# Expert down product with its operands exchanged, the gate on token rows, and attention values 65 columns wide

## Chip, cores, metric

One Trainium2 chip, one of its cores. The metric is the device time of one execution in microseconds (us), the median of the runs.

## The reference, cut to what matters

The program is two transformer layers on `x` of 32 samples × 256 tokens × 128 features, float32. The change is in the first one.

```python
# first attention: 16 query heads, 8 key/value heads of 64
out = jnp.einsum('bhgij,bhjd->bhid', attn, v)      # attn is a causal softmax
# first feed-forward: 16 experts of 64, top 4, and a shared expert of 256
def body(acc, inp):
    wu, wd, cw = inp
    y = relu2(x2 @ wu.T) @ wd.T
    return (acc + cw[:, None] * y, None)
routed, _ = jax.lax.scan(body, jnp.zeros_like(x2), (up_w, down_w, combine.T))
shared = relu2(x2 @ shared_up.T) @ shared_down.T
# and around it, gb being one value per sample and feature
x = x + gb * (routed + shared)
```

`relu2` is the square of relu, `combine` holds a token's weights for its four experts and zero for the others.

## The kernel before

`x` stays in SBUF for the whole program, token rows on the 128 partitions, 64 tiles of 128 tokens. Five stages follow one another, each a block in which every engine runs its own hand-written instruction list; between two blocks all engines meet. The stages are a setup, the first attention, the experts (`moe`), the second attention and an MLP. Semaphores order the engines inside a block.

**Experts.** The loop goes over 16 runs of two samples, 512 tokens. The 1024 hidden features of the 16 experts and the 256 of the shared expert are ten blocks of 128 (`RT` = 8 routed, `ST` = 2 shared), called units u = 0 to 9, the shared ones first. For each unit PE makes the up product into `pU` (512 token columns, `pe_up`, L1093), ACT takes relu into `r` (L1312) and squares it into `a` for a shared unit or `q` for a routed one (L1325). DVE multiplies `q` with the tokens' routing weights `cwB` into `a` (`dve_weigh`, L1238). PE then adds the down product of `a` into `pD` over all ten units (`pe_down`, L1103): the turned-down weights `dT` are loaded, `a` passes with its 512 columns, and `pD` holds features on partitions, tokens in columns. ACT scales `pD` with the gate, a value per feature and sample (`act_gate`, L1332), into `og`; PE turns `og` back to token rows in four transposes into `pB` (`pe_back`, L1110); DVE adds `pB` to `x` (`dve_add`, which calls `add_to_x`, L122) and measures mean and variance for the next layer.

The order of the work is written out by hand in the block of each engine, three runs interleaved: PE does up and down products of run n alternately (down follows up by three units), the last three down products of run n − 1 between the first three up products of run n, then the transposes of run n + 2 (`pe_front`, L1076), the router's product of run n + 2 (`pe_route`, L1084, eight passes) and `pe_back` of n − 1. `pe_down` of unit 0 waits for the gate of the run before, which frees `pD`.

**Routing weights.** DVE computes the weights of run n + 1 (`dve_scores` to `dve_weights`) and turns them into `cwT`. SP stores `cwT` to DRAM (`by_expert`, four stores, L1058), waits for them, and loads them back in four transfers of 512 KB that repeat every expert's row over 64 partitions (`cwB`, L1065). A run's store waits until the load of the run before has landed. SP issues every transfer of this stage; at its start it first calls `ahead`, which issues the ten loads of the later MLP's weights (`mlp_load`, L1813 to L1817).

**First attention.** For each sample, group of four heads and query tile, PE multiplies the softmax numerators `pr` (loaded, 128×128) with the values `va` (passing), whose columns are 64 values, then ones that give the row sum: `VW` = 66 columns, of which the last is a second one that nobody reads (`pe_weighted_values`, L450 and L451). DVE divides by the sum (`dve_outputs`).

A float32 matmul of the program is two matmul instructions in the trace, each with a weight load.

Of the kernel before, what the change touches and what calls it, by code (L numbers as in the profile page):

```python
# [14 lines left out]
P = 128  # L15
# [252 lines left out]
def attention0(nc, c, weights, later, following):  # L268
# [3 lines left out]
    with ExitStack() as ctx:  # L272
# [8 lines left out]
        VW = DH + 2  # L281
# [718 lines left out]
def moe(nc, c, weights, ahead, halve, following, products):  # L1000
# [3 lines left out]
    with ExitStack() as ctx:  # L1004
# [32 lines left out]
        og = sb('og', [D, W])  # L1037
# [8 lines left out]
        s_pz, s_pk, s_pT, s_pd, s_pm = (sem(x) for x in ('pz', 'pk', 'pT', 'pd', 'pm'))  # L1046
        block = ctx.enter_context(nc.Block())

        @block.sync
        def _(sp):  # L1050
            ahead(sp)
            for n in range(RUNS):
                sp.wait_ge(s_cT, n + 1)
                if n >= 1:
                    for part in s_cw:
                        sp.wait_ge(part, 2 * 16 * n)
                for j in range(P // SQ):
                    sp.dma_start(by_expert[:, :, j, :], cwT[SQ * j:SQ * j + E, :, :]).then_inc(s_cd, 16)  # L1058
                sp.wait_ge(s_cd, 16 * P // SQ * (n + 1))
                if n >= 2:  # L1060
                    sp.wait_ge(s_a, RT * (n - 1))
                rows = by_expert.rearrange('(k j y) t g r -> k y j (t g r)', k=2, y=2)
                for k in range(2):
                    for y in range(2):
                        sp.dma_start(cwB[n % 2][EI * y:EI * (y + 1), RT // 2 * k:RT // 2 * (k + 1), :],  # L1065
                                     rows[k, y].unsqueeze(0).broadcast_to((EI, RT // 2, W))).then_inc(s_cw[k], 16)

        def weights_of(u):
            return RT + u if u < ST else u - ST
# [25 lines left out]
        def pe_down(pe, n, u):  # L1095
            if u < ST:
                pe.wait_ge(s_sq, IT * n + u + 1)
            else:
                pe.wait_ge(s_a, RT * n + u - ST + 1)
            if u == 0 and n >= 1:  # L1100
                pe.wait_ge(s_og, n)
            t = weights_of(u)
            pe.matmul(pD[:, :], dT[:, t * D:(t + 1) * D], a[(IT * n + u) % 4][:, :], start=u == 0, stop=u == IT - 1).then_inc(s_dn, 1)  # L1103

        def pe_back(pe, n):
            pe.wait_ge(s_og, n + 1)
            if n >= 1:
                pe.wait_ge(s_st, ADD_STEPS * (n - 1) + 1)
            for t in range(T4):
                last = pe.transpose(pB[:, t * P:(t + 1) * P], og[:, t * P:(t + 1) * P], c.id32[:, :])  # L1110
            last.then_inc(s_oT, 1)

        @block.tensor
        def _(pe):
            for n in range(-2, RUNS + 1):
# [27 lines left out]
                if 0 <= n - 1 < RUNS:  # L1143
                    pe_back(pe, n - 1)
# [94 lines left out]

        def dve_add(dve, n):  # L1240
            dve.wait_ge(s_oT, n + 1)
            add_to_x(dve, c, s_st, n, T4, pB[:, :])
# [5 lines left out]
        def _(dve):  # L1248
            dve.wait_ge(weights.s_loaded, 16 * MOE_LOADS)
            dve.wait_ge(s_km, 4)  # L1250
            for n in range(-2, RUNS + 1):
# [10 lines left out]
                elif n == -1:  # L1262
                    dve_normalise(dve, 2)
                elif 1 <= n < RUNS - 2:
                    dve_normalise(dve, n + 2)
                if 0 <= n < RUNS:
# [60 lines left out]
        def act_gate(act, n):  # L1327
            if n >= 1:
                act.wait_ge(s_oT, n)
            act.wait_ge(s_dn, IT * (n + 1))  # L1330
            for m in range(S2):
                last = act.activation(og[:, m * N:(m + 1) * N], pD[:, m * N:(m + 1) * N], ACT.Copy, scale=c.mod[:, 0, 5, n * S2 + m:n * S2 + m + 1])  # L1332
            last.then_inc(s_og, 1)

        @block.scalar
        def _(act):
            for n in range(-2, RUNS + 1):
# [6 lines left out]
                if 0 <= n - 1 < RUNS:  # L1344
                    act_gate(act, n - 1)
# [862 lines left out]
```

## Time and profile before

| | us |
|---|---|
| median of 3 runs | 2060.88 (2057.25 to 2062.87) |
| profiled execution, its own time | 2060.06 |
| its span in the profile | 2058.3 |
| PE busy | 1982.2 |
| DVE busy | 1661.7 |
| ACT busy | 1432.7 |
| POOL busy | 634.5 |
| mean granted TensorE clock | 0.982 of full |

Busy times are of the profiled execution and its span; the time of an execution is what the device took for it, 1.8 us more than the span here. PE is the matmul engine (PEld its weight loads), DVE the vector engine, ACT the activation engine, POOL the general one, SP the one that issues transfers. Busy time of matmuls is modelled, as they overlap each other; what a matmul costs is read from start to start. In a timeline a row is a group of like instructions: start, length until the last has ended, engine, line, operation, output <- inputs, shapes, count, and in brackets how long the engine was idle before and what ended that.

### The profile page before, as it was taken

The page shows a single profiled execution, that of the slowest core. Times are in us where ns is not written, and L with a number is a line of the kernel's source. Part 1 is how long each engine was busy: PE and PEld are TensorE (multiplying, and loading weights), DVE is VectorE, ACT ScalarE, POOL GpSimd, SP SyncE. Part 2 cuts the span into 40 slices and gives each one's busy share as a digit, 9 for nine tenths or more (in the row PEclk, how much of TensorE's full clock was granted, in tenths as well). Part 3 has the DMA queues.
Part 4 walks back from the last instruction along what each step waited for, and adds up shares of the span by engine and source line. Part 5 has one row for each costly group of instructions (what it writes and reads, how often), then busy time and mean ns, then how long its engine had stood idle before and what let it go on. Part 6 is the DMA issues. An engine that isn't in the chain of part 4 may idle for free. (4 is left out here: it accounts for less than half of the span.)

```text
span 2058.3 us, 39519 instructions
## 1 busy us (share of the span) xinstructions
PE 1982.2 (96%) x14373; PEld 1323.9 (64%) x14373; DVE 1661.7 (81%) x3939; ACT 1432.7 (70%) x1922; POOL 634.5 (31%) x865
## 2 busy tenths in 40 slices
PE   5999999999999999999799999899999997999998
PEld 3777777777777777777444444577777773444443
DVE  5898889888888889874576676588888887999997
ACT  3877878788877888776477777567767764555554
POOL 2444554455444554453000000144444440000000
PEclk9999999999999999999799999999999997999999
DMA  2400000000000000000665455000000000000000
GB/s 88 108 20 21 22 22 11 22 22 22 12 21 22 22 21 12 22 21 11 140 125 123 103 109 124 1 2 2 2 2 2 2 2 1 16 11 17 11 17 16
DMA packets 55360, 69.33 MB, mean 34 GB/s; under 512 B 13009, under 2 KB 32641, under 8 KB 55169
## 3 DMA queue, kind: packets, MB, share of 16 engines
q1 hardware_dynamic: 55168, 66.82, 14.1%
q8 instruction: 116, 1.90, 0.4%
q14 instruction: 76, 0.61, 0.1%
HBM read 45.30 MB, written 4.72 MB: 24 GB/s over the span
## 5 line engine op out<-in xcount | busy, mean ns | idle before, releaser
L904 POOL TENSOR_SCALAR_AFFINE_SELECT pr<-pr 128x512 f32<-128x512 f32 x256 | 201.8, 812 | 371.5 <-ACT pr L827 371.5
L450 PE MATMUL a_pO<-va,pr 128*128 128x66 f32 x2048 | 303.2, 271 | 1.9 <-POOL pr L904 1.5
L450 PEld LDWEIGHTS a_pO<-va,pr 128*128 128x128 f32 x2048 | 272.3, 192 | 18.9 <-issue 15.4
L1736 ACT ACTIVATE c_pr<-c_pS 128x1536 f32<-128x1536 f32 x128 | 185.9, 1453 | 93.8 <-PE c_pS L1543 93.8
L1783 POOL TENSOR_SCALAR_AFFINE_SELECT c_pr<-c_pr 128x512 f32<-128x512 f32 x256 | 176.3, 718 | 212.2 <-DVE c_pr L1635 212.2
L793 ACT ACTIVATE sq<-a_pW 128x512 f32<-128x512 f32 x192 | 114.4, 597 | 148.5 <-PE a_pW L391 145.9
L821 ACT ACTIVATE th<-a_pS 128x1536 f32<-128x1536 f32 x128 | 186.0, 1453 | 30.1 <-PE a_pS L435 29.6
L451 PE MATMUL a_pO<-va,pr 128*128 128x66 f32 x1024 | 198.2, 275 | 0.0
L827 ACT ACTIVATE pr<-th 128x1536 f32<-128x1536 f32 x128 | 190.7, 1490 | 3.0
L435 PE MATMUL a_pS<-qs,k 128*128 128x512 f16 (+1 forms) x1024 | 187.3, 326 | 1.0 <-issue 1.0
L1103 PE MATMUL b_pD<-b_a,b_dn 128*128 128x512 f32 x320 | 165.3, 600 | 5.2 <-DVE b_a L1238 4.8
L1635 DVE TENSOR_SCALAR c_pr<-c_pr 128x1536 f32<-128x1536 f32 x128 | 130.2, 1017 | 47.6 <-ACT c_pr L1736 45.2
L1093 PE MATMUL b_pU<-b_hT,b_un 128*128 128x512 f32 x320 | 167.6, 607 | 0.0
L435 PEld LDWEIGHTS a_pS<-qs,k 128*128 128x128 f16 x1024 | 98.6, 98 | 99.9 <-issue 36.0
L1238 DVE TENSOR_TENSOR b_a<-b_q,b_cwB 128x512 f32<-128x512 f32 x128 | 87.9, 688 | 84.2 <-ACT b_q L1325 79.1
L451 PEld LDWEIGHTS a_pO<-va,pr 128*128 128x128 f32 x1024 | 155.7, 192 | 0.0
L1312 ACT ACTIVATE b_r<-b_pU 128x512 f32<-128x512 f32 x160 | 95.7, 598 | 80.1 <-PE b_pU L1093 80.1
L912 POOL TENSOR_TENSOR as<-on 128x128 f32<-128x128 f32 x256 | 116.9, 467 | 109.9 <-PE a_pW L472 95.5
L687 POOL TENSOR_TENSOR qp<-qg,qp 128x1024 f16<-128x1024 f32 x64 | 137.0, 2142 | 20.1 <-ACT qp L803 20.1
L678 DVE RECIPROCAL rl<-a_pO 128x4 f32<-128x4 f32 x256 | 44.9, 175 | 121.5 <-PE a_pO L451 121.5
L626 DVE TENSOR_TENSOR qg<-a_pW,a_gam 128x512 f32<-128x512 f32 x192 | 131.5, 686 | 10.5 <-ACT sq L793 7.8
L391 PE MATMUL a_pW<-a_wq,hT 128*128 128x512 f32 x256 | 126.8, 619 | 0.7 <-DVE qs L695 0.7
(242 smaller groups left out, 4354.1 us busy)
## 6 DMA issues: line engine op xcount, KB each, us to landing
b_cwB<-b_by_expert SPq DMA_DIRECT2D x64, 512.0 KB, 8.5
k<-k SPq DMA_DIRECT2D x64, 256.0 KB, 3.7
x<-in_L_attn_tokens_dram SPq DMA_DIRECT2D x8, 512.0 KB, 7.3
out_dram<-x SPq DMA_DIRECT2D x16, 256.0 KB, 2.3
d_h<-in_L_ffn_h_w_dram SPq DMA_DIRECT2D x2, 1024.0 KB, 7.3
b_by_expert<-b_cwT SPq DMA_DIRECT2D x64, 8.0 KB, 1.8
wmod<-in_L_wmod_dram SPq DMA_DIRECT2D x2, 384.0 KB, 3.8
d_w<-in_L_ffn_w_w_dram SPq DMA_DIRECT2D x3, 256.0 KB, 3.0
```

The costliest lines, as they stand in the source:

```text
L435: last = pe.matmul(out, kk[:, h // G2, keys * P:(keys + 1) * P], qs[k][:, h:h + G2, keys * P:N], start=first, stop=not first)
L450: pe.matmul(out, w[:, hh * N + t * P:hh * N + (t + 1) * P], v[:, 0, p, :], start=True, stop=t == 0)
L451: last = pe.matmul(out, w[:, HPG * N + hh * P:HPG * N + (hh + 1) * P], v[:, 1, p, :], start=False, stop=True)
L626: dve.tensor_tensor(qg[n % 2][:, t, cols], pW[BANK_OF[m]][:, :], gam[:, cols], ALU.mult).then_inc(s_qg, 1)
L687: eng.tensor_tensor(to[:, t, :, DH:2 * DH], x.rearrange('p (h d) -> p h d', d=DH), to[:, t, :, 0:DH], ALU.subtract).then_inc(done, 1)
L821: act.activation(th[:, :], pS[:, :], ACT.Tanh, scale=1.0 / SOFTCLAMP).then_inc(s_th, 1)
L827: act.activation(pr[g % 2][:, :], th[:, :], ACT.Exp, scale=SOFTCLAMP * DH ** (-0.5)).then_inc(s_pr, 1)
L904: last = gp.affine_select(out=part, in_=part, compare_op=ALU.is_ge, fill=0.0, base=0, pattern=[[0, HPG], [1, P]], channel_multiplier=-1)
L1093: pe.matmul(pU[(IT * n + u) % 4][:, :], uT[:, t, :], hT[n % 3][:, :], start=True, stop=True).then_inc(s_up, 1)
L1103: pe.matmul(pD[:, :], dT[:, t * D:(t + 1) * D], a[(IT * n + u) % 4][:, :], start=u == 0, stop=u == IT - 1).then_inc(s_dn, 1)
L1736: act.activation(pr[g][:, :, :], pS[:, :, 0:N + P], ACT.Exp, scale=float(1.0 / np.sqrt(np.float32(DQ)))).then_inc(s_ex, 1)
L1783: last = gp.affine_select(out=part, in_=part, compare_op=ALU.is_ge, fill=0.0, base=0, pattern=[[0, HPG], [1, P]], channel_multiplier=-1)
```

## The change

- `VW` is 65: the values have one column of ones.
- `pe_down` now loads a block of `a` (128 hidden features × 128 tokens) and passes the 128 columns of `dT`, four times per unit, one for each tile of 128 tokens. `pD` thus holds token rows on partitions, as `x` does. `pe_back` and its transposes are gone.
- The gate is then different in every column and the same on all partitions of a sample. `dve_gate` multiplies `pD` with `gb`, the gates of all 32 samples repeated on every partition (16 KB each), into `og`; `act_gate` is gone, and `dve_add` reads `og`.
- `gb` is made at the start of the stage: PE turns the gates (`pe_turn_gates`), ACT copies them (`act_take_gates`), SP stores them to DRAM (`by_sample`, 16 KB) and loads them back repeated over 128 partitions (2 MB). That load and the MLP's ten loads (`ahead`) are issued in run 0 behind the load of its routing weights.

```diff
-        VW = DH + 2
+        VW = DH + 1
...
-        og = sb('og', [D, W])
+        og = sb('og', [P, T4, D])
+        gs_, gb = sb('gates', [B, D]), sb('gb', [P, B, D])
+        by_sample = nc.dram_tensor('b_by_sample', (B, D), F32, kind='Internal').ap()
...
         @block.sync
         def _(sp):
-            ahead(sp)
+            sp.wait_ge(s_gs, 1)
+            sp.dma_start(by_sample, gs_[:, :]).then_inc(s_gd, 16)
             for n in range(RUNS):
...
+                if n == 0:
+                    sp.wait_ge(s_gd, 16)
+                    sp.dma_start(gb[:, :, :].rearrange('p b d -> p (b d)'),
+                                 by_sample.rearrange('b d -> (b d)').partition_broadcast(P)).then_inc(s_gb, 16)
+                    ahead(sp)
...
-            t = weights_of(u)
-            pe.matmul(pD[:, :], dT[:, t * D:(t + 1) * D], a[(IT * n + u) % 4][:, :], start=u == 0, stop=u == IT - 1).then_inc(s_dn, 1)
-
-        def pe_back(pe, n):
-            pe.wait_ge(s_og, n + 1)
-            if n >= 1:
-                pe.wait_ge(s_st, ADD_STEPS * (n - 1) + 1)
+            rows = weights_of(u)
             for t in range(T4):
-                last = pe.transpose(pB[:, t * P:(t + 1) * P], og[:, t * P:(t + 1) * P], c.id32[:, :])
-            last.then_inc(s_oT, 1)
+                last = pe.matmul(pD[:, t * P:(t + 1) * P], a[(IT * n + u) % 4][:, t * P:(t + 1) * P], dT[:, rows * D:(rows + 1) * D],
+                                 start=u == t == 0, stop=u == IT - 1, skip_group_check=True)
+            last.then_inc(s_dn, 1)
+
+        def pe_turn_gates(pe):
+            pe.transpose(pB[0:B, 0:D], c.mod[:, 0, 5, :], c.id32[:, :]).then_inc(s_gT, 1)
...
+        def dve_gate(dve, n):
+            dve.wait_ge(s_dn, IT * (n + 1))
+            if n == 0:
+                dve.wait_ge(s_gb, 16)
+            else:
+                dve.wait_ge(s_st, ADD_STEPS * (n - 1) + 1)
+            by = gb[:, n * S2:(n + 1) * S2, :].unsqueeze(2).broadcast_to((P, S2, TT, D))
+            dve.tensor_tensor(og[:, :, :].rearrange('p (s t) d -> p s t d', s=S2),
+                              pD[:, :].rearrange('p (s t d) -> p s t d', s=S2, t=TT), by, ALU.mult).then_inc(s_og, 1)
+
         def dve_add(dve, n):
-            dve.wait_ge(s_oT, n + 1)
-            add_to_x(dve, c, s_st, n, T4, pB[:, :])
+            dve.wait_ge(s_og, n + 1)
+            add_to_x(dve, c, s_st, n, T4, og[:, :, :].rearrange('p t d -> p (t d)'))
...
+                if 0 <= n - 1 < RUNS:
+                    dve_gate(dve, n - 1)
                 if 0 <= n < RUNS:
                     dve_weigh(dve, n, 2)
...
-        def act_gate(act, n):
-            if n >= 1:
-                act.wait_ge(s_oT, n)
-            act.wait_ge(s_dn, IT * (n + 1))
-            for m in range(S2):
-                last = act.activation(og[:, m * N:(m + 1) * N], pD[:, m * N:(m + 1) * N], ACT.Copy, scale=c.mod[:, 0, 5, n * S2 + m:n * S2 + m + 1])
-            last.then_inc(s_og, 1)
+        def act_take_gates(act):
+            act.wait_ge(s_gT, 1)
+            act.activation(gs_[:, :], pB[0:B, 0:D], ACT.Copy).then_inc(s_gs, 1)
```

The instruction lists at three places. Line numbers above 1034 are 3 to 17 higher after the change.

SP at the start of the expert stage, before: the ten MLP loads (`d_w`, `d_h` and their scales; six of them left out), then run 0's stores and loads of routing weights and run 1's stores.

```order
L1813 DMA d_w<-in_L_ffn_w_w_dram 128x4x128
L1814 DMA d_w1s<-in_L_ffn_w_s_dram 128x4x1
...
L1816 DMA d_w<-in_L_ffn_w_w_dram 128x512
L1817 DMA d_w3s<-in_L_ffn_w_s_dram 128x1
L1058 DMA b_by_expert<-b_cwT 64x1x32 [waits b_cT]
L1058 DMA b_by_expert<-b_cwT 64x1x32 x3
L1065 DMA b_cwB<-b_by_expert 64x4x512 [waits b_cd]
L1065 DMA b_cwB<-b_by_expert 64x4x512 x3
L1058 DMA b_by_expert<-b_cwT 64x1x32 [waits b_cw1,b_cw0,b_cT]
```

After:

```order
L1054 DMA b_by_sample<-b_gates 32x128 [waits b_gs]
L1061 DMA b_by_expert<-b_cwT 64x1x32 [waits b_cT]
L1061 DMA b_by_expert<-b_cwT 64x1x32 x3
L1068 DMA b_cwB<-b_by_expert 64x4x512 [waits b_cd]
L1068 DMA b_cwB<-b_by_expert 64x4x512 x3
L1072 DMA b_gb<-b_by_sample 128x4096 [waits b_gd]
L1825 DMA d_w<-in_L_ffn_w_w_dram 128x4x128
...
L1829 DMA d_w3s<-in_L_ffn_w_s_dram 128x1
L1061 DMA b_by_expert<-b_cwT 64x1x32 [waits b_cw1,b_cw0,b_cT]
```

The MLP's loads moved from ahead of run 0's routing weights to between those of run 0 and of run 1, with the gates' load in front of them.

PE at the turn from one run to the next, before: from the last down product of a run to the third of the next.

```order
L1103 MATMUL b_pD<-b_a,b_dn 128x512 [waits b_a]
L1076 MATMUL b_pX<-id,b_xn 128x128 [waits b_hT,b_xn]
L1076 MATMUL b_pX<-id,b_xn 128x128 x3
L1093 MATMUL b_pU<-b_hT,b_un 128x512 [waits b_r]
L1103 MATMUL b_pD<-b_a,b_dn 128x512 [waits b_og,b_sq]
...
L1084 MATMUL b_pR<-b_gT,b_hT 128x16 [waits b_ex,b_hT]
L1084 MATMUL b_pR<-b_gT,b_hT 128x16 x3
L1093 MATMUL b_pU<-b_hT,b_un 128x512 [waits b_r]
L1110 MATMUL b_pB<-id,b_og 128x128 [waits b_st,b_og]
L1110 MATMUL b_pB<-id,b_og 128x128 x3
L1103 MATMUL b_pD<-b_a,b_dn 128x512 [waits b_a]
```

After:

```order
L1112 MATMUL b_pD<-b_dn,b_a 128x128 [waits b_a]
L1112 MATMUL b_pD<-b_dn,b_a 128x128 x3
L1084 MATMUL b_pX<-id,b_xn 128x128 [waits b_hT,b_xn]
L1084 MATMUL b_pX<-id,b_xn 128x128 x3
L1101 MATMUL b_pU<-b_hT,b_un 128x512 [waits b_r]
L1112 MATMUL b_pD<-b_dn,b_a 128x128 [waits b_og,b_sq]
L1112 MATMUL b_pD<-b_dn,b_a 128x128 x3
...
L1092 MATMUL b_pR<-b_gT,b_hT 128x16 [waits b_ex,b_hT]
L1092 MATMUL b_pR<-b_gT,b_hT 128x16 x3
L1101 MATMUL b_pU<-b_hT,b_un 128x512 [waits b_r]
L1112 MATMUL b_pD<-b_dn,b_a 128x128 [waits b_a]
```

Each down product is four narrow ones, with the wait ahead of the first; the four transposes into `pB` are gone; the wait for `og` stays at the first down product of a run.

DVE at the same turn, before: the end of the routing weights, the normalised tokens `xn`, the weighing of u = 2 to 4 and the residual add.

```order
L1230 STREAM_TRANSPOSE b_cwT<-b_cwp 128x128 [waits b_cd,b_rt]
L112 TENSOR_SCALAR b_xn<-x,mv,rs 128x128 [waits b_xT]
L112 TENSOR_SCALAR b_xn<-x,mv,rs 128x128 x3
L1238 TENSOR_TENSOR b_a<-b_q,b_cwB 128x512 [waits b_dn,b_cw0,b_sq] x3
L122 TENSOR_TENSOR x<-x,b_pB 128x512 [waits b_oT]
```

After:

```order
L1235 STREAM_TRANSPOSE b_cwT<-b_cwp 128x128 [waits b_cd,b_rt]
L112 TENSOR_SCALAR b_xn<-x,mv,rs 128x128 [waits b_xT]
L112 TENSOR_SCALAR b_xn<-x,mv,rs 128x128 x3
L1252 TENSOR_TENSOR b_og<-b_pD,b_gb 128x512 [waits b_st,b_dn]
L1243 TENSOR_TENSOR b_a<-b_q,b_cwB 128x512 [waits b_dn,b_cw0,b_sq] x3
L122 TENSOR_TENSOR x<-x,b_og 128x512 [waits b_og]
```

The gate stands between `xn` and the weighing, and waits for the last down product.

## Rows read from the trace of the kernel before

**Rows 1.** The page, busy time of each engine with its share of the span
```profile
PE 1982.2 (96%) x14373; PEld 1323.9 (64%) x14373; DVE 1661.7 (81%) x3939; ACT 1432.7 (70%) x1922; POOL 634.5 (31%) x865
```

**Rows 2.** Windows, a steady run: length, busy, clock, DMA share, GB/s
```profile
1096.73:1115.69 18.96, 18.96 (x57) 9.19 (x56) 13.19 (x57) 14.10 (x27) 0.00 (x0) 1.00 0.53 114
```

**Rows 3.** Timeline of PE, run 0: start, length, instruction, count, idle before
```profile
1007.58 2.07 PE L1103 MATMUL b_pD<-b_a,b_dn 128*128 128x512 f32 x2 [4.79 <-DVE b_a L1238]
```

**Rows 4.** Timeline of DVE, run 0 of the experts
```profile
1006.84 2.50 DVE L1238 TENSOR_TENSOR b_a<-b_q,b_cwB 128x512 f32<-128x512 f32 x4 [4.41 <-DMA b_cwB<-b_by_expert]
```

**Rows 5.** Timeline of SP's DMA issues, start of the expert stage
```profile
981.62 0.39 SPq L1813 DMA_DIRECT2D d_w<-in_L_ffn_w_w_dram  x1
...
995.21 2.57 SPq L1058 DMA_DIRECT2D b_by_expert<-b_cwT  x4
999.02 2.61 SPq L1065 DMA_DIRECT2D b_cwB<-b_by_expert  x4
1011.71 2.49 SPq L1058 DMA_DIRECT2D b_by_expert<-b_cwT  x4
1015.45 2.58 SPq L1065 DMA_DIRECT2D b_cwB<-b_by_expert  x4
```

**Rows 6.** Timeline of PE within a steady run
```profile
1103.29 1.02 PE L1103 MATMUL b_pD<-b_a,b_dn 128*128 128x512 f32 x2
1104.15 0.96 PE L1084 MATMUL b_pR<-b_gT,b_hT 128*128 128x16 f32 x8
1104.96 1.10 PE L1093 MATMUL b_pU<-b_hT,b_un 128*128 128x512 f32 x2
1105.90 0.60 PE L1110 MATMUL b_pB<-id,b_og 128*128 128x128 f32 x4
1106.34 0.59 PE L1103 MATMUL b_pD<-b_a,b_dn 128*128 128x512 f32 x1
```

**Rows 7.** Timeline of PE in the first attention, weighted values
```profile
602.38 0.61 PE L450 MATMUL a_pO<-va,pr 128*128 128x66 f32 x4
602.83 0.39 PE L451 MATMUL a_pO<-va,pr 128*128 128x66 f32 x2
```

**Rows 8.** Timeline of PE in the second attention, value product
```profile
1314.42 0.61 PE L1530 MATMUL c_pB<-c_wv,c_hT 128*128 128x128 f32 x4
1314.86 0.55 PE L1844 MATMUL c_pS<-id,d_w 128*128 128x128 f16 x7
```

**Rows 9.** Timeline of DVE at the turn of a steady run
```profile
1101.90 0.69 DVE L1238 TENSOR_TENSOR b_a<-b_q,b_cwB 128x512 f32<-128x512 f32 x1 [2.08 <-ACT b_q L1325]
```

**Rows 10.** Timeline of ACT at the same place
```profile
1100.51 0.84 ACT L1332 ACTIVATE b_og<-b_pD,mod 128x256 f32<-128x256 f32 x2 [0.32 <-PE b_pD L1103]
```

**Rows 11.** Timeline of PE, end of the expert stage
```profile
1304.56 0.27 PE L1432 MATMUL b_pU<-id,c_dkv 128*32 128x128 f32 x1
```

**Rows 12.** Timeline of ACT, end of the expert stage
```profile
1305.44 0.36 ACT L1437 ACTIVATE c_dT<-b_pU 32x256 f32<-32x256 f32 x1
```

**Rows 13.** Timeline of DVE, run 1 of the experts
```profile
1025.07 0.69 DVE L1238 TENSOR_TENSOR b_a<-b_q,b_cwB 128x512 f32<-128x512 f32 x1 [2.76 <-ACT b_q L1325]
```

**Rows 14.** Timeline of PE, run 1 of the experts
```profile
1029.54 1.02 PE L1103 MATMUL b_pD<-b_a,b_dn 128*128 128x512 f32 x2
```

**Rows 15.** Windows of the start, the MLP load, routing load, wait's end
```profile
8.00:10.00 2.00, 1.06 (x6) 0.95 (x6) 0.95 (x5) 0.00 (x0) 0.00 (x0) 1.00 0.95 368
...
980.00:996.00 16.00, 9.36 (x29) 6.50 (x30) 9.84 (x52) 3.94 (x10) 2.25 (x11) 0.59 0.64 182
999.00:1010.00 11.00, 6.21 (x18) 3.02 (x17) 6.21 (x28) 3.91 (x9) 0.00 (x0) 0.85 0.90 185
...
1007.60:1013.40 5.80, 5.80 (x7) 2.50 (x8) 3.33 (x8) 1.23 (x2) 0.00 (x0) 0.50 0.51 99
```

**Rows 16.** DMA in 982 to 996: 40 slices' busy tenths; a load's landing
```profile
DMA  0057997999768999999667999999999864210000
...
d_w3s<-in_L_ffn_w_s_dram SPq DMA_DIRECT2D x1, 0.5 KB, 6.6
```

More of the change, by code:

```diff
@@ L1045, in moe @@
         s_og, s_oT, s_st = (sem(x) for x in ('og', 'oT', 'st'))
-        s_pz, s_pk, s_pT, s_pd, s_pm = (sem(x) for x in ('pz', 'pk', 'pT', 'pd', 'pm'))
+        s_gT, s_gs, s_gd, s_gb, s_pz, s_pk, s_pT, s_pd, s_pm = (sem(x) for x in ('gT', 'gs', 'gd', 'gb', 'pz', 'pk', 'pT', 'pd', 'pm'))
         block = ctx.enter_context(nc.Block())
@@ L1101, in pe_down @@
                 pe.wait_ge(s_og, n)
-            t = weights_of(u)
-            pe.matmul(pD[:, :], dT[:, t * D:(t + 1) * D], a[(IT * n + u) % 4][:, :], start=u == 0, stop=u == IT - 1).then_inc(s_dn, 1)
-        def pe_back(pe, n):
-            pe.wait_ge(s_og, n + 1)
-            if n >= 1:
-                pe.wait_ge(s_st, ADD_STEPS * (n - 1) + 1)
-            for t in range(T4):
-                last = pe.transpose(pB[:, t * P:(t + 1) * P], og[:, t * P:(t + 1) * P], c.id32[:, :])
-            last.then_inc(s_oT, 1)
+            rows = weights_of(u)
+            for t in range(T4):
+                last = pe.matmul(pD[:, t * P:(t + 1) * P], a[(IT * n + u) % 4][:, t * P:(t + 1) * P], dT[:, rows * D:(rows + 1) * D],
[3 more added lines that the diff above has]
+            pe.transpose(pB[0:B, 0:D], c.mod[:, 0, 5, :], c.id32[:, :]).then_inc(s_gT, 1)
         @block.tensor
         def _(pe):
+            pe_turn_gates(pe)
             for n in range(-2, RUNS + 1):
@@ L1142, in _ @@
                     pe_up(pe, n, 5)
-                if 0 <= n - 1 < RUNS:
-                    pe_back(pe, n - 1)
                 if n == RUNS:
@@ L1325, in act_square @@
             act.activation(to[:, :], r[(IT * n + u) % 4][:, :], ACT.Square).then_inc(s_sq, 1)
-        def act_gate(act, n):
-            if n >= 1:
-                act.wait_ge(s_oT, n)
-            act.wait_ge(s_dn, IT * (n + 1))
-            for m in range(S2):
-                last = act.activation(og[:, m * N:(m + 1) * N], pD[:, m * N:(m + 1) * N], ACT.Copy, scale=c.mod[:, 0, 5, n * S2 + m:n * S2 + m + 1])
-            last.then_inc(s_og, 1)
+        def act_take_gates(act):
+            act.wait_ge(s_gT, 1)
+            act.activation(gs_[:, :], pB[0:B, 0:D], ACT.Copy).then_inc(s_gs, 1)
         @block.scalar
         def _(act):
+            act_take_gates(act)
             for n in range(-2, RUNS + 1):
@@ L1343, in _ @@
                     act_relu(act, n, 2)
-                if 0 <= n - 1 < RUNS:
-                    act_gate(act, n - 1)
                 if n == RUNS:
```

## The prediction

> **What bounds the kernel now.** I read the page first, then the stretches of the program, then PE, DVE, ACT and the DMA queue where the change works. TensorE is busy 96% of the span, no other engine over 81% [rows 1]. One steady run of the expert stage (two samples) takes 18.96 us, all of it PE busy, beside 13.2 us of DVE and 14.1 us of ACT [rows 2]. So in the steady part only PE's own passes count. The exception is the stage's start: in run 0 PE stands 4.79 us before the down product of u = 2 [rows 3], because DVE stands 4.41 us for the broadcast of the routing weights, `b_cwB` [rows 4]. That load is issued at 999.02 [rows 5] and lets DVE begin at 1006.84, 7.8 us later; PE follows 0.74 us behind.
>
> A float32 product is two passes, each with its own weight load. Two 512-column passes take 1104.15 − 1103.29 = 0.86 us [rows 6]. The router's eight 16-column passes and the two wide ones behind them take 1105.90 − 1104.15 = 1.75 us, so the eight cost 0.89, or 0.111 each, though 16 columns need almost nothing: the weight load sets their pace. Passes of 66 columns go at the same pace, four in 0.45 us [rows 7]. The nearest row for 128 moving columns, each pass with its own 128×128 float32 block, is the value product of the second attention: four passes in 1314.86 − 1314.42 = 0.44 us, again 0.11 each [rows 8].
>
> **The change part by part.**
>
> Values 65 columns wide. 3072 passes in the first attention lose one of 66 columns. Their pace is the load's, so I take 0. Were they paced by columns, each would lose 1/66 of 0.112 = 1.7 ns, 5.2 us in all: the bound on the gain side. A loss would need the moving half of a pass (65 columns at 0.43/512 = 0.055 us) to double before it shows; an odd row start is in no row here, so I keep +1 us for it.
>
> Down product turned over. Ten units per run now go as four products of 128 columns with `a` loaded: eight passes, 0.89 us in place of 0.86, +0.03 × 160 = +5 us. The four transposes of `og` leave PE: 1106.34 − 1105.90 = 0.44 us a run [rows 6], −7 us. Net **−2 us**. The wait ahead of each unit stays where it was, and held the load up before too.
>
> The gate. ACT's two activations go; DVE gets one 512-element multiply out of PSUM, for which I take the 0.69 us of its other 512-element operations. DVE was free at 1099.82 and then idle for 2.08 us [rows 9]; PSUM is complete at about 1100.5, when ACT began its 0.84 us [rows 10]. So the gate would end at 1101.2, where ACT's ended at 1101.35. PE asks for that release after four transposes and an up product, 0.44 + 0.86 us behind the last down product, at about 1101.5: hidden, with 0.3 us of cover. Queued behind it on DVE is the weighing of u = 2, which began at 1101.90 when ACT's square let it; that square now comes up to 0.8 us sooner. The residual add reads SBUF, no longer waits for PE, and costs the same 0.69. All this at 0. If the cover failed, PE would wait in 15 runs.
>
> The tail. In the last run the transposes for the following stage end at 1304.8 [rows 11], and ACT's copy of them starts at 1305.44, behind the gate [rows 12]. It now starts at their end, and PE's small products and ACT's last copies, the chain to the stage's end, move up by that: **−0.7 us**.
>
> Start of the stage: a transpose of the gates, an ACT copy and a 16 KB store, all done well before SP's first store of routing weights at 995.21 [rows 5]: 0.
>
> **The DMA queue** is where I expect a cost. All transfers are issued by SP into one queue. Before, the MLP weights went out from 981.62 on, ahead of the first routing weights [rows 5]. Now SP issues them behind `b_cwB` of run 0, and between the two a new 2 MB broadcast of the gates. Run 1's stores come only after. They went out at 1011.71 and their load at 1015.45, 3.74 us later [rows 5], for a DVE operation at 1025.07 [rows 13], where 1015.45 + 7.8 = 1023.3 was early enough. PE takes that run's down product u = 2 at 1029.54 [rows 14].
>
> The queue's work in the new order: `b_cwB` of run 0, 2.1 MB, fills 0.90 of 999 to 1010, 9.9 us of work, and drains at about 1010.2 [rows 15]. Then the gates, also 2.1 MB. Bounds: 10 us, as `b_cwB`, whose transfers each reach 64 partitions; or 5.7 us at 368 GB/s, what the queue moves at 8 to 10 us, when the first attention's weights, a broadcast to all 128 partitions among them, come in [rows 15]. The gates have that second shape, so 5.7: until 1015.9. Then the MLP weights: in 980 to 996 they fill 0.64, 10.2 us of work [rows 15]; from first to last packet it was 34 slices of 0.35 us, 12 us [rows 16]; between the two I take 11.1: until 1027.0. Whatever SP issues meanwhile stands behind: a 0.5 KB load at the end of that burst took 6.6 us to land [rows 16]. Run 1's stores then land about 1.3 us later (3.74 less the 2.5 us of issuing four), its load goes out near 1028.3, DVE begins 7.8 us later at 1036.1 and PE at 1036.8, against 1029.5: **+7.3 us**. With both lower ends (5.7 and 10.2) it is +6.4, with both upper ones (10 and 12) +12.5.
>
> The clock. Behind the wait of 4.79 us the granted clock is 0.50 (1.2 GHz) for the 5.8 us from 1007.6, all of it PE busy [rows 15]: work of 2.9 us took 5.8. A longer wait should do the same again: **+2.9 us**. Later runs recover: run 2's load would go out about 1028.3 + 10.6 + 3.7 = 1042.6 (10.6 until all of run 1's has landed, as in run 0) and free DVE at 1050.4, its product being due near 1058.
>
> Of this queue the Trainium skill ("DMA: Bandwidth & Descriptors", queues, rings and completion order) says that each DMA engine takes up the descriptors of one ring in ring order. By that rule the later stores cannot overtake; the landing of the 0.5 KB load agrees.
>
> Sum: −2 − 0.7 + 7.3 + 2.9 = +7.5 against the profiled execution's own 2060.06 us. That execution lies 0.8 us under the median of 2060.88, inside the scatter of the runs (2057.25 to 2062.87), so I predict the median plus 7.5, rounded: **2068.5 us**. What a measurement here can tell from no change is 0.3%, 6.2 us.
>
> **Rivals.**
>
> *The queue is empty in time* (20%). Run 1's weights let DVE begin by 1028.8, because the burst drains sooner than its parts say. Then 2060.9 − 2.7 = 2058.2 us, no measurable change. For it: 18 us lie between the end of run 0's load and that need. Against it: 7.8 of them are run 1's own load, and 10 do not hold 5.7 + 10.2.
>
> *The gate on DVE comes late* (8%). If it overruns its cover by 0.3 us, 15 runs pay that: 4.5 us more, 2073 us. For it: one engine waits for PSUM with the next weighing behind it. Against: 2.08 us of idle time at the place.
>
> *Loads not hidden* (3%). If a load of `a` could not run beside the passes before it, each of 1280 passes would cost load plus move, 0.107 (a quarter of 0.43) more: +137 us, near 2205. The value product speaks against it: unhidden, its four passes would take 0.87 us, not 0.44. The Trainium skill ("TensorE: Matmul & The Clock Gate", packing small matmuls) states that a weight load overlaps matmuls in flight only when its row group differs; all 128 rows are in use here, and the trace disagrees.
>
> *The other side: narrow passes are cheaper* (5%). Each ns by which the down passes go below 0.111 us is worth 1.28 us. From 0.100 us down this gain (14 us) outweighs the queue by more than 6.2 us and the kernel is faster; at 0.095 us it is 2068.5 − 16 × 1.28 = 2048 us. Against it: neither 128, 66 nor 16 columns made a float32 load of 128 columns faster in any row. The Trainium skill ("TensorE: Matmul & The Clock Gate", back-to-back issue gap) gives about 81 ns per matmul of 128 columns in a sustained stream; by it the time would be 2068.5 − 30 × 1.28 = 2030 us, an estimate from that page that the rows contradict.
>
> **How the numbers follow.** The forecast has 0.6, other drift the last 0.04. The forecast's own range is 2067.6 to 2073.7. The range over all goes down to the case without a wait and up past the queue's upper bounds: **2057.5 to 2075**. Slower by over 6.2 us: most of the forecast (0.45), late gate and unhidden loads, 0.56. Within 6.2 us: the forecast's lower edge, the empty queue and half the drift, 0.36 rounded down. Faster: 0.08.
>
> **What would show it.** In the new profile: eight down passes of 128 columns in 0.89 us; a steady run of about 18.8 us, PE without idle; run 1's `b_cwB` issued near 1028 instead of 1015; a second PE wait of about 7 us near 1030 with the clock at half behind it; no change in the first attention's length. I am wrong if that second wait is absent, or if the steady run is not within 0.2 us of 18.8.

## The result and the profile after

| | before | changed | ratio, 95% interval |
|---|---|---|---|
| first measurement, medians of 20 runs each | 2058.34 us | 2063.48 us | 1.0019 [1.0011, 1.0028] |
| repeated beside later experiments, medians of 23 and 6 | 2056.32 us | 2064.73 us | 1.0041 [1.0026, 1.0055] |
| profiled execution | 2060.06 us (span 2058.3) | 2064.41 us (span 2062.4) | |

The ratios of this study are of all the runs; the quotient of the first two medians is 1.0025, +5.1 us. The change costs 3.9 us by the first ratio (0.0019 × 2058; 2.3 to 5.8 by its interval) and 8.4 by the second (5.3 to 11.3), where +7.5 was forecast. The first lies within 0.3%: by it the outcome is "no difference", not the forecast's "slower". The range held the time.

The page of the changed kernel, against [rows 1] and, for the gates' load, the part on DMA issues:

```profile
PE 1980.9 (96%) x15270; PEld 1402.8 (68%) x15270; DVE 1668.9 (81%) x3955; ACT 1422.9 (69%) x1891; POOL 634.1 (31%) x865
...
L1112 PE MATMUL b_pD<-b_dn,b_a 128*128 128x128 f32 x1280 | 171.1, 278 | 4.6 <-DVE b_a L1243 4.5
...
b_gb<-b_by_sample SPq DMA_DIRECT2D x1, 2048.0 KB, 14.6
```

PE is busy 1.3 us *less* (1982.2 to 1980.9), yet the span grew by 4.1. So PE works no longer than before, and something is waited for. The timeline of PE across runs 0 to 2 (start, length, instruction, count, idle before) shows where. (The transposes `b_pX` are made a run and more ahead: those at 1028.39 are for run 3, and run 1's products go on behind them.)

```profile
1006.66 2.08 PE L1112 MATMUL b_pD<-b_dn,b_a 128*128 128x128 f32 x8 [4.53 <-DVE b_a L1243]
...
1021.94 1.05 PE L1112 MATMUL b_pD<-b_dn,b_a 128*128 128x128 f32 x8
1028.39 1.11 PE L1084 MATMUL b_pX<-id,b_xn 128*128 128x128 f32 x4 [5.40 <-DVE b_xn L112]
1029.30 1.91 PE L1101 MATMUL b_pU<-b_hT,b_un 128*128 128x512 f32 x2
...
1034.70 0.96 PE L1092 MATMUL b_pR<-b_gT,b_hT 128*128 128x16 f32 x8
1035.51 1.10 PE L1101 MATMUL b_pU<-b_hT,b_un 128*128 128x512 f32 x2
1036.45 1.05 PE L1112 MATMUL b_pD<-b_dn,b_a 128*128 128x128 f32 x8
...
1050.70 0.66 PE L1084 MATMUL b_pX<-id,b_xn 128*128 128x128 f32 x4 [0.93 <-DVE b_xn L112]
```

The same transposes in the kernel before:

```profile
997.01 0.60 PE L1076 MATMUL b_pX<-id,b_xn 128*128 128x128 f32 x4
...
1023.48 0.60 PE L1076 MATMUL b_pX<-id,b_xn 128*128 128x128 f32 x4
...
1043.34 0.66 PE L1076 MATMUL b_pX<-id,b_xn 128*128 128x128 f32 x4 [0.76 <-DVE b_xn L112]
```

The wait in run 0 is that of [rows 3], 4.53 us now. There is a second long one, 5.40 us, but at another instruction than forecast: before the transposes at 1028.39, in front of run 1's products u = 0 and 1, not before u = 2. The timeline of DVE names what DVE itself waited for there:

```profile
1027.03 0.31 DVE L1235 STREAM_TRANSPOSE b_cwT<-b_cwp 128x128 f32<-128x128 f32 x1 [6.92 <-DMA b_by_expert<-b_cwT]
1027.26 1.07 DVE L112 TENSOR_SCALAR b_xn<-x,mv,rs 128x128 f32<-128x128 f32 x4
1028.25 0.68 DVE L1252 TENSOR_TENSOR b_og<-b_pD,b_gb 128x512 f32<-128x512 f32 x1
1034.93 1.89 DVE L1243 TENSOR_TENSOR b_a<-b_q,b_cwB 128x512 f32<-128x512 f32 x3 [5.99 <-issue]
```

`cwT` is a single buffer. Before DVE may write run 2's routing weights into it, run 1's have to be stored, and those stores stand in the queue behind the gates and the MLP weights. The tokens `xn` are queued behind that transpose on DVE, and PE waits for `xn`. The second DVE wait, 5.99 us, ends 8.0 us after the issue of run 1's `b_cwB` at 1026.95, and so by its landing, as I read it. (The view says "issue" here; run 0's load took 7.8 us from issue to DVE's start [rows 4, 5], and the experiment with two `cwT` below has the same wait with the load named.) The timeline of SP's issues:

```profile
981.60 0.34 SPq L1054 DMA_DIRECT2D b_by_sample<-b_gates  x1
994.52 2.57 SPq L1061 DMA_DIRECT2D b_by_expert<-b_cwT  x4
998.36 2.61 SPq L1068 DMA_DIRECT2D b_cwB<-b_by_expert  x4
1001.01 1.21 SPq L1072 DMA_DIRECT2D b_gb<-b_by_sample  x1
...
1003.29 7.91 SPq L1825 DMA_DIRECT2D d_w<-in_L_ffn_w_w_dram  x1
...
1018.72 0.64 SPq L1829 DMA_DIRECT2D d_w3s<-in_L_ffn_w_s_dram  x1
1019.46 2.64 SPq L1061 DMA_DIRECT2D b_by_expert<-b_cwT  x4
1026.95 2.58 SPq L1068 DMA_DIRECT2D b_cwB<-b_by_expert  x4
```

Against [rows 5], run 1's stores went out at 1019.46 instead of 1011.71 and its load at 1026.95 instead of 1015.45. Of these 11.5 us, 7.75 are the stores' later issue, for SP stood in the issues before them (7.91 us in one), and 3.75 their slower landing: 7.49 us from their issue to the load's, against 3.74. Now the windows, columns as in [rows 15]: the gates' load, the half clock behind the new wait, the stretch behind that, and a steady run.

```profile
1010.50:1015.50 5.00, 5.00 (x26) 3.81 (x26) 2.36 (x11) 2.79 (x5) 0.00 (x0) 0.78 0.98 389
1026.00:1033.00 7.00, 4.61 (x15) 3.58 (x16) 1.91 (x6) 1.75 (x4) 0.00 (x0) 0.53 0.67 146
1033.00:1040.00 7.00, 7.00 (x41) 5.00 (x41) 4.48 (x11) 3.99 (x8) 0.00 (x0) 0.99 0.76 153
...
1088.45:1107.30 18.85, 18.85 (x114) 14.07 (x113) 13.69 (x57) 13.50 (x25) 0.00 (x0) 1.00 0.54 114
```

The steady run takes 18.85 us against 18.96 [rows 2], still all PE. The first timeline answers to [rows 6] (PE), the second to [rows 9] (DVE):

```profile
1103.80 1.02 PE L1101 MATMUL b_pU<-b_hT,b_un 128*128 128x512 f32 x2
1104.66 1.05 PE L1112 MATMUL b_pD<-b_dn,b_a 128*128 128x128 f32 x8
1105.55 1.02 PE L1101 MATMUL b_pU<-b_hT,b_un 128*128 128x512 f32 x2
```

```profile
1107.50 0.69 DVE L1252 TENSOR_TENSOR b_og<-b_pD,b_gb 128x512 f32<-128x512 f32 x1 [0.48 <-PE b_pD L1112]
```

The eight passes take 1105.55 − 1104.66 = 0.89 us. The tail, PE's timeline, against [rows 11]:

```profile
1309.99 0.27 PE L1444 MATMUL b_pU<-id,c_dkv 128*32 128x128 f32 x1
...
1314.39 1.86 PE L1856 MATMUL c_pS<-id,d_h 128*128 128x128 f16 x16 [2.57 <-PEq L1004]
```

From these starts the stage can be cut into four pieces, and every profile of this study with it. The cuts are the first `b_pX` transposes, those for run 2, those for run 4 (these are the two runs hit by the queue), the small `c_dkv` transpose, and the first product of the next stage.

| us | start | two runs | both | rest | tail | stage |
|---|---|---|---|---|---|---|
| before | 12.59 | 46.33 | 58.92 | 261.22 | 5.29 | 325.43 |
| changed | 12.52 | 54.43 | 66.95 | 259.29 | 4.40 | 330.64 |
| difference | −0.1 | +8.1 | **+8.0** | −1.9 | −0.9 | +5.2 |
| changed, repeated | 12.40 | 54.63 | 67.03 | 259.29 | 4.41 | 330.73 |

"Both" is the start and the two runs together, and is the column to compare kernels by. In four of the eleven profiles the start is 0.8 us shorter, but run 0's down product of u = 2 comes no sooner for it: from the stage's first transposes to it are 22.6 to 23.2 us in every profile. A short start only lengthens the wait for run 0's weights, which counts among the two runs.

What lies outside the stage was 0.9 us shorter in the changed kernel's profiled execution (2064.41 − 330.64 against 2060.06 − 325.43). Over all eleven profiled executions it was 1728.5 to 1736.2 us, with no order by kernel: that is scatter, and I attribute nothing to it. The pieces of the stage repeat far better: changed and repeated within 0.2 us each.

### The profile page after: what moved, and what is told of

Same layout as the page of the kernel before. It is cut to its first block and busy times, and to the rows that moved or that the text cites. A ratio compares the mean times of both kernels' runs of the same rounds, so it can differ in the third digit from the quotient of the medians.

```text
span 2062.4 us, 41285 instructions
## 1 busy us (share of the span) xinstructions
PE 1980.9 (96%) x15270; PEld 1402.8 (68%) x15270; DVE 1668.9 (81%) x3955; ACT 1422.9 (69%) x1891; POOL 634.1 (31%) x865
## 5 line engine op out<-in xcount | busy, mean ns | idle before, releaser
L450 PE MATMUL a_pO<-va,pr 128*128 128x65 f32 x2048 | 302.5, 270 | 1.9 <-POOL pr L904 1.5
L1112 PEld LDWEIGHTS b_pD<-b_dn,b_a 128*128 128x128 f32 x1280 | 169.9, 194 | 82.1 <-issue 65.4
L451 PE MATMUL a_pO<-va,pr 128*128 128x65 f32 x1024 | 198.0, 275 | 0.0
L1112 PE MATMUL b_pD<-b_dn,b_a 128*128 128x128 f32 x1280 | 171.1, 278 | 4.6 <-DVE b_a L1243 4.5
## 6 DMA issues: line engine op xcount, KB each, us to landing
b_gb<-b_by_sample SPq DMA_DIRECT2D x1, 2048.0 KB, 14.6
```

Of the source, the lines that this page charges most:

```text
L450: pe.matmul(out, w[:, hh * N + t * P:hh * N + (t + 1) * P], v[:, 0, p, :], start=True, stop=t == 0)
L451: last = pe.matmul(out, w[:, HPG * N + hh * P:HPG * N + (hh + 1) * P], v[:, 1, p, :], start=False, stop=True)
L1112: last = pe.matmul(pD[:, t * P:(t + 1) * P], a[(IT * n + u) % 4][:, t * P:(t + 1) * P], dT[:, rows * D:(rows + 1) * D], start=u == t == 0, ...
```

## The experiments

**MLP weights back at the front.** The changed kernel, with one line moved. The gates' load stays where the change put it.

```diff
+            ahead(sp)                      # stage's start, before the wait for the gates
             sp.wait_ge(s_gs, ...)
...
                 if n == 0:
                     sp.dma_start(gb ...)
-                    ahead(sp)
```

> The changed kernel with the MLP's ten loads issued first in the expert stage, as before the change; the gates' load stays behind the routing weights of run 0. Theory (the queue): run 1's stores wait for the gates' 2 MB alone, land near 1017, PE's idle time before the transposes of run 3 shrinks from 5.40 us to under 0.5, no second stretch at half clock, and the kernel is 3 us faster than before the change (0.15 us a run and 0.9 us of tail gained, nothing paid). Rival (the cost lies in the gate on DVE or in the narrow passes): still 4 to 5 us slower than before, like the changed kernel.

2053.14 us against 2055.02, ratio 0.9986 [0.9977, 0.9995]. Run 1's `b_cwB` went out at 1016.50 and DVE waited for nothing at the transpose of `cwT`:

```profile
1019.62 0.31 DVE L1235 STREAM_TRANSPOSE b_cwT<-b_cwp 128x128 f32<-128x128 f32 x1
...
1025.42 1.29 DVE L1243 TENSOR_TENSOR b_a<-b_q,b_cwB 128x512 f32<-128x512 f32 x2 [2.21 <-DMA b_cwB<-b_by_expert]
```

This is 2.9 us less than before, where 3 was expected. Start and two runs take 58.54 us, against 58.92 before and 66.95 in the changed kernel; the stage takes 322.23. So the whole cost of the change is the place of the MLP loads together with the gates' load, and without it the change gains. Its 2.21 us of DVE wait no longer reaches PE.

**Gates' load early, MLP weights late.** The changed kernel, the other half.

```diff
+            sp.wait_ge(s_gd, 16)           # right behind the store of the gates
+            sp.dma_start(gb ...)
...
                 if n == 0:
-                    sp.wait_ge(s_gd, 16)
-                    sp.dma_start(gb ...)
                     ahead(sp)
```

> The changed kernel with the gates' load issued right behind the store of the gates, in the idle queue at the stage's start; the MLP's loads stay behind the routing weights of run 0. Theory (the queue, costs add by its work): run 1's stores then stand behind the MLP's loads alone, some 5 to 6 us less than in the changed kernel, and land near 1022; PE idles 0.5 to 1 us instead of 5.40 before the transposes of run 3; the time is 2 us less to 1 us more than before. Rival (the gates' load is harmless, the MLP's loads make the whole wait): the idle time stays over 4 us and the kernel 4 us slower than before.

2056.73 against 2055.02, ratio 1.0004 [0.9994, 1.0014]. Run 1's stores went out at 1016.63, its load at 1023.81. Start and two runs: 60.81, +1.9 against before. The time is as expected, but PE's wait is not where I expected it. DVE waits at the transpose of `cwT` and again at the weighing; PE feels only the second wait, 0.98 us before u = 2 of run 1, and none before the transposes of run 3. The timelines of DVE and then PE:

```profile
1023.88 0.31 DVE L1235 STREAM_TRANSPOSE b_cwT<-b_cwp 128x128 f32<-128x128 f32 x1 [1.52 <-DMA b_by_expert<-b_cwT]
...
1031.39 1.90 DVE L1243 TENSOR_TENSOR b_a<-b_q,b_cwB 128x512 f32<-128x512 f32 x3 [5.42 <-DMA b_cwB<-b_by_expert]
```

```profile
1032.14 1.16 PE L1112 MATMUL b_pD<-b_dn,b_a 128*128 128x128 f32 x8 [0.98 <-DVE b_a L1243]
```

The two moves don't add. By start and two runs, and in the changed kernel, the gates' load in place alone makes −0.4 us (nothing lost, and the work of two runs a little cheaper), the MLP loads alone +1.9, both +8.0. As I read it, each alone is taken up in whole or in part by the slack between run 0's load and run 1's need, and together they are past it; how long that slack is was not measured by itself.

**The MLP loads moved in the kernel before.** Nothing else of the change.

```diff
-            ahead(sp)                      # stage's start
...
                 sp.dma_start(cwB[n % 2] ...)
+                if n == 0:
+                    ahead(sp)
```

> The kernel before with the MLP's ten loads moved behind run 0's routing weights and nothing else changed. Theory (the queue's work adds up): these loads alone take 11 us of the queue, run 1's stores land near 1022.5 and its weights let DVE begin near 1031; PE idles 1 us once, runs 0 and 1 take 2 us longer together, and the kernel is 1 to 3 us slower than before. Rival (the MLP's loads are most of the cost): 4 us or more slower.

2060.78 against 2056.32, ratio 1.0019 [1.0008, 1.0030]: +3.9 us. The profile's start and two runs take 61.47, +2.6. By the time this is more than I had expected, though its interval (1.6 to 6.2 us) reaches down to it; by the profile it is inside my 1 to 3. The stores are late here too and hold DVE at the transpose of `cwT` for 1.44 us, but PE has work meanwhile. Its wait lies where the prediction had looked for it, before u = 2 of run 1. DVE, then PE:

```profile
1025.11 0.31 DVE L1231 STREAM_TRANSPOSE b_cwT<-b_cwp 128x128 f32<-128x128 f32 x1 [1.44 <-DMA b_by_expert<-b_cwT]
```

```profile
1034.18 1.12 PE L1104 MATMUL b_pD<-b_a,b_dn 128*128 128x512 f32 x2 [1.42 <-DVE b_a L1239]
```

**Only the values 65 wide.** The kernel before, `VW = DH + 1`.

> The kernel before with the attention's values 65 columns wide and nothing else changed. Theory (a float32 pass is paced by its weight load): the same time within 0.5 us, 0.112 us a pass as before. Rival (columns count, 1/66 of a pass): 5 us faster. Second rival (odd rows are read more slowly): slower.

2057.11 against 2055.02, ratio 1.0007 [0.9997, 1.0017]: nothing that can be told. The groups of the first attention (60 to 960 us) show why, here of this kernel and then of the one before:

```profile
L450 PE MATMUL a_pO<-va,pr 128*128 128x65 f32 x2016 | 297.7, 270 | 0.4 <-DVE on L682 0.4
```

```profile
L450 PE MATMUL a_pO<-va,pr 128*128 128x66 f32 x2014 | 297.8, 270 | 0.4 <-DVE on L682 0.4
```

The same 270 ns each, and four passes in 0.45 us, as in [rows 7]. The stage of this kernel takes 325.29 us, as before.

**A second buffer for the transposed weights.** The changed kernel with two `cwT`, so that DVE never waits for the stores of the run just before.

```diff
-        cwp, cwT = (sb(x, [P, T4, SQ]) for x in ('cwp', 'cwT'))
+        cwp = sb('cwp', [P, T4, SQ])
+        cwT = [sb(f'cwT{k}', [P, T4, SQ]) for k in range(2)]
...
-            if n >= 1:
-                dve.wait_ge(s_cd, 16 * P // SQ * n)
+            if n >= 2:
+                dve.wait_ge(s_cd, 16 * P // SQ * (n - 1))
```

> The changed kernel with two buffers for the turned routing weights, so that DVE's transpose of run 2's weights no longer waits for run 1's stores. Theory (the wait for the stores only came first; behind it the routing weights of run 1 bound all, at DVE 1034.9 and PE 1036.4): PE's 5.40 us of idle time before the transposes of run 3 vanish and come back before the down product of u = 2 of run 1, some 6 us long, and the stretch at half clock now lies behind the wait instead of beside it, so that the kernel is no faster and up to 3 us slower than the changed one. Rival (the wait for the stores is itself the cost): 5 us faster than the changed kernel.

2065.77 against 2055.02, ratio 1.0046 [1.0033, 1.0059]; start and two runs 67.13. The wait at the transposes is gone and the cost is not, as expected. I ran it again beside a repeat of the changed kernel, to see if it was worse than that one or only as bad.

> The changed kernel once more, on the same chip as the next three. Theory: 3 to 6 us slower than before; runs 0 and 1 of the experts (transposes of run 2 to those of run 4) take 8 us more than before, every steady run 18.85 us.

> Two buffers for the turned routing weights once more, beside the changed kernel on one chip. Theory (the half clock lies beside the wait in the changed kernel and behind it here): 1 to 5 us slower than the changed kernel, PE's long idle time ahead of the down product of u = 2 in run 1, and the products behind it at half clock. Rival (the earlier difference was scatter): the same time as the changed kernel within 1 us. Rival (the wait for the stores costs by itself): faster than the changed kernel.

Changed: 2064.73, ratio 1.0041 [1.0026, 1.0055]. That is 8.4 us over before and outside the 3 to 6 expected, though the interval (5.3 to 11.3) reaches into them; its two runs are 8.3 us longer, as expected. Two buffers: 2064.58, ratio 1.0043 [1.0029, 1.0057]. The same as the changed kernel, and not 1 to 5 us slower: the rival that called the earlier difference scatter was right. DVE's second wait with two buffers, and then PE's timeline:

```profile
1036.04 1.90 DVE L1244 TENSOR_TENSOR b_a<-b_q,b_cwB 128x512 f32<-128x512 f32 x3 [12.02 <-DMA b_cwB<-b_by_expert]
```

```profile
1023.13 0.60 PE L1085 MATMUL b_pX<-id,b_xn 128*128 128x128 f32 x4
...
1036.79 2.07 PE L1113 MATMUL b_pD<-b_dn,b_a 128*128 128x128 f32 x8 [7.80 <-DVE b_a L1244]
1038.65 1.55 PE L1102 MATMUL b_pU<-b_hT,b_un 128*128 128x512 f32 x2
1040.04 1.05 PE L1113 MATMUL b_pD<-b_dn,b_a 128*128 128x128 f32 x8
...
1052.16 0.66 PE L1085 MATMUL b_pX<-id,b_xn 128*128 128x128 f32 x4 [0.56 <-DVE b_xn L112]
```

This is the picture that the prediction had drawn: no wait at the transposes, then 7.80 us before u = 2 of run 1, with half clock *behind* it (the eight passes from 1036.79 take 1.86 us until the next product, against 0.89, and that one 1.39 against 0.86; from 1040.04 on the pace is full). The slow clock thus costs 1.5 us here, and 1.9 in the first profile of this kernel (three groups from 1034.81 to 1039.38, 4.57 us against 2.64), not the 2.9 of the prediction. So the end of the two runs is set by the arrival of run 1's weights and what the clock adds behind it. Without the store wait PE does the same work sooner and then stands longer. The store wait itself costs nothing: start and two runs take 66.95 and 67.03 us with one buffer, 67.13 and 67.52 with two, and the times don't tell the two apart.

**Spreading the loads.** With the cause known, can more be had? Gates' load first, then the MLP weights in four parts in runs 2 to 5 instead of in one burst.

```diff
-                    ahead(sp)
+                if 2 <= n <= 5:
+                    ahead(sp, n - 2)       # w1 and w2; h1; h2; w3
```

> The changed kernel with the gates' load issued first and the MLP's loads spread over runs 2 to 5 behind each run's routing weights (two small ones, h1, h2, the rest), their halving moved two runs later. Theory (nothing big stands ahead of run 1's stores): runs 0 and 1 together as long as with the MLP's loads first (46.8 us) or up to 1 us shorter, no idle time ahead of the transposes of run 4; 3 to 5 us faster than before, the fastest of all. Rival (a load of 1 MB behind a run's weights makes the next run's late in its turn): PE idle time before a down product in runs 3 to 6.

2053.30 against 2056.32, ratio 0.9986 [0.9975, 0.9997]; start and two runs 58.85, stage 322.53. This is 2.9 us faster than before, at the edge of the 3 to 5 expected, and no better than the MLP weights at the front (58.54): with either order run 1's weights come in time, and the start's own wait of about 5 us for run 0's remains. The wait ahead of the transposes of run 4, which I had expected to go, is still there, 0.92 us. The rival's waits in runs 3 to 6 did not come.

**Run 0's weights through two queues.** The same, with the loads of partitions 64 to 127 of run 0's `cwB` issued by ACT.

```diff
-                    for y in range(2):
+                    for y in range(2 if n else 1):
...
+                    act.dma_start(cwB[0][EI:P, ...], rows[k, 1] ...)
```

> The kernel with the spread loads (e8), where in run 0 alone ACT issues the two loads of routing weights that go to partitions 64 to 127, beside SP's two for partitions 0 to 63. Theory (a load that reaches 64 partitions moves 210 GB/s, one that reaches all 128 about 390, so both halves at once should move about 390): DVE begins the weighing of run 0 some 2 us sooner, PE idles 2.5 to 3.5 us before it instead of 4.7, and the kernel is 1 to 3 us faster than e8. Rival (what holds the load at 210 GB/s is the repeated reading of the same DRAM rows): the same time as e8.

2052.77 against 2056.01, ratio 0.9988 [0.9977, 0.9998]. The load did not get faster: from its first issue at 996.82 to DVE's start at 1005.00 it took 8.2 us, against 7.6 in the spread kernel. Window of its transfer, and PE's waits in run 0:

```profile
1000.00:1005.00 5.00, 2.02 (x10) 1.19 (x10) 0.22 (x1) 3.36 (x8) 0.00 (x0) 0.85 1.03 222
```

```profile
1000.52 1.07 PE L1092 MATMUL b_pR<-b_gT,b_hT 128*128 128x16 f32 x8 [2.08 <-ACT b_hT L1318]
...
1005.75 2.08 PE L1112 MATMUL b_pD<-b_dn,b_a 128*128 128x128 f32 x8 [3.21 <-DVE b_a L1243]
```

3.21 + 2.08 is no less than the 4.5 to 5.5 us of the other kernels: PE's 2.08 us wait for ACT's `hT`, behind ACT's two issues, took up what the other wait gave back. Both halves are on their way at once here and the rate is still 222 GB/s, so my idea that transfers to 64 partitions are slow because they reach only half of them falls. (The Trainium skill, "DMA: Bandwidth & Descriptors", rules for kernel authors, says that two transfers to disjoint partition halves share the same engines either way. The trace agrees in so far as the rate stayed at 222 GB/s.)

All stages in one table:

| us | start | two runs | both | rest | tail | stage | ratio |
|---|---|---|---|---|---|---|---|
| MLP first | 11.74 | 46.80 | 58.54 | 259.29 | 4.40 | 322.23 | 0.9986 |
| gates first | 12.64 | 48.17 | 60.81 | 259.29 | 4.40 | 324.50 | 1.0004 |
| before, 65 wide | 12.52 | 46.26 | 58.78 | 261.22 | 5.29 | 325.29 | 1.0007 |
| before, MLP late | 12.59 | 48.88 | 61.47 | 261.22 | 5.29 | 327.98 | 1.0019 |
| two `cwT` | 11.73 | 55.40 | 67.13 | 259.30 | 4.40 | 330.83 | 1.0046 |
| two `cwT`, again | 11.74 | 55.78 | 67.52 | 259.32 | 4.40 | 331.24 | 1.0043 |
| spread | 12.35 | 46.50 | 58.85 | 259.29 | 4.39 | 322.53 | 0.9986 |
| two queues | 11.74 | 46.81 | 58.55 | 259.29 | 4.40 | 322.24 | 0.9988 |

The start is 11.7 us in some and 12.4 to 12.6 in others. This goes with the pace of the first `b_pX` transposes, which take 0.7 us where it is short and 1.1 where it is long (1.09 in all for the second set), whatever the kernel; the same four take 0.60 at the full clock. "Rest" and "tail" are the price of the new down product and gate, and are the same to 0.03 us wherever these are in. "Both" shows what a kernel pays in the queue: within 0.4 us of the 58.92 before, or 1.9 and 2.6 us above it, or 8.2 and 8.6.

## Why the prediction was right and wrong

**Where it failed: the sum "7.3 + 2.9".** The clock's term of 2.9 us was added on top of the wait. In the changed kernel the stretch at half clock (granted 0.53 in 1026 to 1033) lay beside the wait for `b_cwB`, not behind it. PE worked from 1028.39 to 1036.45; at full pace, with rows of 0.44 (transposes), 0.86 (up, three), 0.89 (down, two) and 0.89 (router), that work is 5.7 us instead of 8.1. But DVE's first weighing ended at 1034.93 + 0.69 = 1035.6 at the earliest, so full pace would have brought u = 2 to about 1035.6 and not to 1034.1: by this estimate the clock cost some 0.8 us, not 2.9. Measured for both terms together: 8.0 us against 10.2, some 0.2 us of cheaper work in these two runs included. With this the stage is +5.2 instead of +7.5. Had the clock stood in the sum with 0.8, the forecast would have been +5.4 us, under the bound of 6.2, and "no difference".

The term was also too large by itself. The runs with two buffers hold the half clock behind the wait, where the prediction had put it, and there it cost 1.9 and 1.5 us. The down product of u = 2 in run 1 came 6.2 and 7.0 us later after the stage's first transposes than before, and start and two runs grew by 8.2 and 8.6, not by 10.2. The 2.9 was taken over from run 0, where the slow stretch was 5.8 us long [rows 15]; behind the wait of 7.12 us it was over after 4.6 us and behind that of 7.80 after 3.3. Why it was shorter, no run shows.

**A wait I had not named.** I had asked what a late load of run 1's weights holds up, and not what their late store does. The single `cwT` makes DVE wait for the store, `xn` wait for DVE and PE for `xn`. It is what moved the idle time ahead of the work at half clock, so that this work lies beside the wait for the weights. It cost nothing itself, as the two buffers show.

**Right, by step.** The queue: gates' load until about 1015.6 (14.6 us from its issue at 1001.01) against 1015.9, at 389 GB/s against the 368 taken; `b_cwB` of run 1 issued at 1026.95 against 1028.3; the product u = 2 of run 1 at 1036.45 against 1036.8, which began at 1029.54 before [rows 14]. (The stage began 0.7 us sooner, so by its own start this is +7.6, of which the clock has some 0.8; the queue's own share is then about 6.8 of the 7.3 forecast.) Later runs recover, as said: the `b_pX` of run 4 waits 0.93 us against 0.76 before, and PE shows no wait from then to the tail. Down products 0.89 us for eight; steady run 18.85 against "about 18.8"; rest of the stage −1.9, against −2 for all 16 runs. Tail −0.9 against −0.7. Values 65 wide: 0. Gate on DVE: it starts at 1107.50, 0.48 us after DVE fell idle, and PE never waits for it; hidden. First attention: no change outside scatter.

**The rivals.** *The queue is empty in time* did not come, and two experiments show how near it was: with the gates' load alone it holds (start and two runs 58.54 against 58.92), with the MLP loads alone it nearly does (60.81). *Gate late*: no. *Narrow passes cheaper*: no, 0.111 us each at the full clock. *Loads not hidden*: no. The Trainium skill has two passages on this in "TensorE: Matmul & The Clock Gate": packing small matmuls, that a load overlaps only if its row group differs, and the steps of a matmul, that a load into the background weight buffer is pulled ahead too. The down passes, with all rows in use, go against the first and fit the second: were load and move one after the other, eight would take 8 × (0.111 + 0.107) = 1.7 us by the prediction's figures, and not 0.89.

**The chances.** A term of 7.5 us beside a bound of 6.2 decides by 1.3 us, and I gave "slower" 0.56. The cost is 3.9 and 8.4 us by two measurements and 5.2 by the stage alone; the two intervals meet at 1.0026 to 1.0028, 5.3 to 5.8 us. So it was the draw of the measurement that decided whether "slower by over 6.2 us" came true. By the second it did, though the stage's own +5.2 would not have borne it out. What makes the two ratios differ, I can't say. The changed kernel's stage was the same in both (330.64 and 330.73); the kernel before was profiled in the first alone, so that the difference lies in the 1730 us outside is likely and not shown.

## What to carry to other kernels

A queue in order makes a bulk load that nobody needs soon into a cost for the small load behind it. So look for the slack of the *next* latency-bound transfer and fill it once: here 2 MB fitted, 2.8 MB cost about 2 us, and both together 8. If a change pushes bulk loads behind the first of a series of small stores, put those that have no dependency ahead of it; this alone turned +0.2 to +0.4% into −0.14% [−0.23, −0.05]. And when two delays are predicted for one place (a wait and a slow clock), draw both on one time line before adding them: here the clock cost some 0.8 us beside the wait and 1.5 to 1.9 behind it.

## What was not expected of the hardware

- Narrow float32 passes, each with its own weight load, all run at 0.111 to 0.112 us, with 16, 65, 66 or 128 moving columns. Exchanging the operands of a product 512 columns wide so that 128 columns move four times then gains nothing by itself (0.89 for 0.86 us here); the gain was the four transposes of 0.44 us that it made needless.
- One issue on SP took 7.91 us (1003.29) while the loads ahead of it were moving, where the same issue at the stage's start took 0.50 (kernel with the MLP weights first). What stands behind it on SP waits as well, though it belongs to other data: run 1's stores went out only at 1019.46.
- 2 MB came in at 389 GB/s as one row of 16 KB repeated to 128 partitions, and 2.1 MB as rows of 2 KB repeated to 64 partitions at 185 GB/s (mean of 11 us, DMA share 0.90 [rows 15]), or 222 (share 1.03) with the issues split over SP and ACT. Whether the row length or the repeated reads do this stays open.
